# Cross attention with transposed scores, its output tiles spread over the iterations

## The reference, cut to what matters

```
def _attn(xq, ctx, wq, wkv, wo, bo):
    q = _heads(xq @ wq)
    k, v = jnp.split(ctx @ wkv, 2, axis=-1)
    ...
    q = _rope(q, sq, cq)
    k = _rope(k, sk, ck)
    sim = jnp.einsum('bhnd,bhmd->bhnm', q, k) * DH ** (-0.5)
    a = jax.nn.softmax(sim, axis=-1)
    o = jnp.einsum('bhnm,bhmd->bhnd', a, v)
    o = o.transpose(0, 2, 1, 3).reshape(xq.shape[0], xq.shape[1], MID)
    return o @ wo + bo
...
cross_in = _adaln(x, cond, ln1_w, ln1_b, g1_w, g1_b, b1_w, b1_b)
ctx_n = _ln(context, ca_lnc_w, ca_lnc_b)
x = _attn(cross_in, ctx_n, ca_wq, ca_wkv, ca_wo, ca_bo) + x
```

## Time and profile before

| what | us |
|---|---|
| median of three runs | 2480.38 |
| profiled execution, its own time | 2478.87 |
| its span | 2477.1 |
| PE busy | 2228.5 (90%) |
| DVE busy | 1860.5 (75%) |
| ACT busy | 1330.3 (54%) |
| POOL busy | 355.7 (14%) |

### The profile page before, as it was taken

One profiled execution on the slowest core, in us unless ns is written; L12 is line 12 of the kernel. 1 busy time (PEld: TensorE's weight loads), 2 busy tenths in 40 slices (PEclk: granted clock), 3 DMA queues, 4 the chain that ended last, 5 costly groups with the idle time before them and its releaser, 6 DMA issues. The chain is left out here.

```text
span 2477.1 us, 40034 instructions
## 1 busy us (share of the span) xinstructions
PE 2228.5 (90%) x15036; PEld 1042.1 (42%) x15036; DVE 1860.5 (75%) x2924; ACT 1330.3 (54%) x1655; POOL 355.7 (14%) x201
## 2 busy tenths in 40 slices
PE   2499999999999999999999999944899999994899
PEld 2133333344333344333334333442465656563566
DVE  6579989877989886899986998574766666666453
ACT  5266666755676654666664666443443443444221
POOL 3100000000000000000000000023554545452000
PEclk9699999999999999999999999967898999986899
DMA  5101010101111011101010110052322222224211
GB/s 163 54 35 36 35 44 35 39 32 44 52 40 40 27 44 44 52 27 44 35 44 35 52 36 27 19 160 72 94 85 85 85 85 85 85 85 128 67 38 34
DMA packets 106254, 143.81 MB, mean 58 GB/s; under 512 B 28209, under 2 KB 74367, under 8 KB 106111
## 3 DMA queue, kind: packets, MB, share of 16 engines
q1 hardware_dynamic: 106111, 141.87, 17.9%
HBM read 55.70 MB, written 12.85 MB: 28 GB/s over the span
## 5 line engine op out<-in xcount | busy, mean ns | idle before, releaser
L642 PE MATMUL sa_ps_o<-sa_probs,sa_v_pair 128*64 128x512 f32 x2048 | 532.7, 614 | 2.9 <-DVE sa_mx L897 2.9
L806 ACT ACTIVATE sa_probs<-sa_ps_s 128x1024 f32<-128x1024 f32 x512 | 495.8, 1025 | 27.9 <-PE sa_ps_s L629 27.9
L897 DVE CUSTOM_DVE_ANT_0 sa_rise<-sa_ps_t,sa_rise 128x512 f32<-128x512 f32 x504 | 327.9, 688 | 190.7 <-PE sa_ps_t L606 190.3
L910 DVE TENSOR_TENSOR sa_acc<-sa_acc,sa_probs 128x1024 f32<-128x1024 f32 x384 | 462.6, 1246 | 7.2 <-ACT sa_probs L806 7.2
L794 ACT ACTIVATE sa_rise<-sa_ps_t 128x1024 f32<-128x1024 f32 x252 | 257.7, 1023 | 250.0 <-PE sa_ps_t L599 250.0
L642 PEld LDWEIGHTS sa_ps_o<-sa_probs,sa_v_pair 128*64 128x64 f32 x2048 | 101.9, 134 | 246.4 <-issue 173.7
L576 POOL TENSOR_TENSOR sa_xr<-sa_xr,sa_bo_row 128x1024 f32<-128x1024 f32 x8 | 21.6, 2726 | 1280.1 <-DMA sa_xr<-in_x 1280.1
L622 PE MATMUL sa_ps_s<-sa_hi 64*128 64x512 f16 x1024 | 194.5, 376 | 0.0
L622 PE MATMUL sa_ps_s<-sa_hi,sa_lo 64*128 64x512 f16 x1024 | 194.4, 376 | 0.0
L622 PE MATMUL sa_ps_s<-sa_lo,sa_hi 64*128 64x512 f16 x1024 | 194.4, 376 | 0.0
L629 PE MATMUL sa_ps_s<-sa_m_line,sa_m_ones 64*128 64x512 f16 x1024 | 189.5, 377 | 3.7 <-DMA sa_m_line<-sa_m_rows 3.7
(11 more groups left out here) (275 smaller groups left out, 4613.5 us busy)
## 6 DMA issues: line engine op xcount, KB each, us to landing
sa_swp<-sa_raw SPq DMA_DIRECT2D x128, 256.0 KB, 2.4
ca_swp<-ca_raw SPq DMA_DIRECT2D x70, 256.0 KB, 2.4
sa_inv<-sa_scratch SPq DMA_DIRECT2D x128, 128.0 KB, 2.9
ca_q_hl<-ca_hi SPq DMA_DIRECT2D x68, 128.0 KB, 2.3
ca_q_hl<-ca_lo SPq DMA_DIRECT2D x68, 128.0 KB, 2.3
sap_xs<-in_x SPq DMA_DIRECT2D x4, 1024.0 KB, 7.1
sa_xr<-in_x SPq DMA_DIRECT2D x4, 1024.0 KB, 5.9
cap_xs<-x_after_self SPq DMA_DIRECT2D x4, 1024.0 KB, 7.2
```

Of the source, the lines that this page charges most:

```text
L642: ins = pe.matmul(ps_o[rows(x), half(c)], v_pair[:, kt, rows(x)], probs[:, kt % 2, c, half(x)], start=(kt == 0), stop=(kt == NK - 1))
L806: act.activation(probs[:, kt % 2, c, :], ps_s[c][:, :], ACT.Exp, scale=float(DH) ** -0.5).then_inc(s_p, 1)
L897: dve.tensor_tensor_reduce(out=larger, in0=max_banks(j, t)[:, half(x)], in1=larger, scale=1.0, scalar=-3.0e38, op0=ALU.add, op1=ALU.max, a ...
L910: dve.tensor_tensor(acc[:, c, :], before, probs[:, kt % 2, c, :], ALU.add).then_inc(s_acc[c], 1)
```

## The change

Cross attention is written anew in 32 unrolled iterations, one for each head pair g. The scores are made with the 77 keys on the partitions, both heads of the pair at once from 64 rows each (`scores`), so that probabilities need no transposing. The maxima come from separate products of the high parts with queries on the partitions (`bases`), one DVE instruction over 1232 columns, one transpose of 128 by 16, and one transfer into four lines; four products of 32 rows subtract them (`shift`). Sums come from four products with ones, and go through `few`, a scratch in memory and two transfers of 256 KB into `inv`; DVE divides the output. The rotation of q is on DVE alone. `swp` has one buffer instead of two. The values of pair g - 1 stand ahead of the transpose of g's maxima. One output tile of the batch before is made in each iteration from g = 11 on, with `o_hi` and `o_lo` two batches deep; three tiles and the last batch's eight follow the iterations. x is loaded and stored tile by tile, and its bias is added by POOL tile by tile. In the context stage the stacking transfers go, and the split keys are written where cross attention reads them; the key and value weights are freed ahead of cross attention.

```diff
-                sp.wait_ge(s_hi, n + 1)
-                for x in range(2):
-                    for dst in (k_hh[0:DH], k_hh[DH:P]):
-                        sp.dma_start(dst[:, half(n), x], hi[DH * x:DH * x + DH, half(n)]).then_inc(s_stack, 16)
-                sp.wait_ge(s_lo, n + 1)
-                for x in range(2):
-                    sp.dma_start(k_lo[:, half(n), x], lo[DH * x:DH * x + DH, half(n)]).then_inc(s_stack, 16)
-            sp.wait_ge(s_stack, 16 * 12)
+                sp.wait_ge(s_swap[n], 32)
...
-        ps_sc = ps("ps_sc", [P, TT, P])
-        ps_pt = ps("ps_pt", [P, N])
+        ps_s = ps("ps_s", [P, 2, N])
         ps_o = ps("ps_o", [P, N])
-        ps_turn = [ps(f"ps_turn{i}", [P, HALF]) for i in range(2)]
+        ps_t = ps("ps_t", [P, N])
+        turn = [ps_t[:, 0:HALF], ps_t[:, HALF:N]]
...
+        def output_tile(g):
+
+            return g - PAIRS - 3 if PAIRS + 3 <= g < PAIRS + 3 + TT * (B - 1) else None
+
+        def y_bank(n):
+            if n < TT * (B - 1):
+                later = n - output_tile(G)
+                return (turn[0] if later <= 0 else ps_s[:, 1, :] if later == 1 else turn[1])[:, 0:D]
+            t = n % TT
+            return (ps_s[:, t // 2, t % 2 * HALF:t % 2 * HALF + D] if t < 4 else turn[t - 4][:, 0:D] if t < 6 else
+                    ps_o[:, (t - 6) * HALF:(t - 6) * HALF + D])
+
+            def line(j):
+                sp.wait_ge(s_mt_r, j + 1)
+                sp.dma_start(m_line[0:P:32, :], m_rows[:]).then_inc(s_line, 16)
+
+            def gather_sums(g):
+                sp.wait_ge(s_sum_r, g + 1)
+                if g >= 1:
+                    sp.wait_ge(s_scr, 16 * g)
+                sp.dma_start(few[:], sums[0:P:32, :]).then_inc(s_few, 16)
+
+            def spread_inverses(g):
+                sp.wait_ge(s_rec, g + 1)
+                if g >= 1:
+                    sp.wait_ge(s_inv, 32 * g)
+                    sp.wait_ge(s_div, g)
+                sp.dma_start(scratch.rearrange("n (i k) -> (n i) k", k=16), few[:]).then_inc(s_scr, 16)
+                sp.wait_ge(s_scr, 16 * (g + 1))
                 for x in range(2):
-                    sp.dma_start(q_hl[0:DH, par, x, :], hi[DH * x:DH * x + DH, :]).then_inc(s_stack[par], 16)
-                sp.wait_ge(s_lo, j + 1)
-                for x in range(2):
-                    sp.dma_start(q_hl[DH:P, par, x, :], lo[DH * x:DH * x + DH, :]).then_inc(s_stack[par], 16)
+                    sp.dma_start(inv[rows(x), :], scratch[2 * x:2 * x + 2].rearrange("a k -> (a k)")
+                                 .partition_broadcast(DH)).then_inc(s_inv, 16)
+
+            def store(n):
+                sp.wait_ge(s_yr, n + 1)
+                sp.dma_start(y_v[n // TT][:, n % TT, :], xr[:, n % TT, :]).then_inc(s_out[n % 2], 16)
+
+            def load(n):
+                sp.wait_ge(s_out[n % 2], 16 * ((n - TT) // 2 + 1))
+                if n >= TT + 2:
+                    sp.wait_ge(s_xb, 2 + n - TT - 1)
+                sp.dma_start(xr[:, n % TT, :], x_v[n // TT][:, n % TT, :]).then_inc(s_x[n % 2], 16)
 
...
+            for g in range(G):
+                if g + 2 < G:
+                    swap(g + 2)
+                line(g)
+                n = output_tile(g - 1)
+                if n is not None:
+                    if n >= 2:
+                        load(n - 2 + TT)
+                    store(n)
+                if g >= 2:
+                    spread_inverses(g - 2)
+                if g >= 1:
+                    gather_sums(g - 1)
+            spread_inverses(G - 2)
+            gather_sums(G - 1)
+            spread_inverses(G - 1)
...
+            for h in range(2):
+                hs = slice(TT // 2 * h, TT // 2 * (h + 1))
+                pool.tensor_tensor(xr[:, hs, :], xr[:, hs, :], bo_row[:].broadcast_to([P, TT // 2, D]),
+                                   ALU.add).then_inc(s_xb, 1)
+            for n in range(TT, TT * B):
+                pool.wait_ge(s_x[n % 2], 16 * ((n - TT) // 2 + 1))
+                pool.tensor_tensor(xr[:, n % TT, :], xr[:, n % TT, :], bo_row[:, 0, :], ALU.add).then_inc(s_xb, 1)
 
...
+            def bases(g):
+                b, pair = g // PAIRS, g % PAIRS
                 for t in range(TT):
-                    ts = slice(t * P, (t + 1) * P)
-                    pe.matmul(ps_sc[:, t, 0:M], q_hl[:, par, x, ts], k_hh[:, pair, x, b, :], start=True, stop=False)
-                    ins = pe.matmul(ps_sc[:, t, 0:M], q_hl[0:DH, par, x, ts], k_lo[:, pair, x, b, :],
-                                    start=False, stop=True)
-                ins.then_inc(s_sc_w, 1)
-
-            def transposes(par, x):
-                for t in range(TT):
-                    ins = pe.transpose(ps_pt[0:M, t * P:(t + 1) * P], e[:, par, x, t, :], ident[:, :])
-                ins.then_inc(s_pt_w, 1)
+                    at = t // 4 * HALF + t % 4 * M
+                    for x in range(2):
+                        ins = pe.matmul(ps_s[:, x, at:at + M],
+                                        hi[rows(x), g % 3, t * P:(t + 1) * P], k_hi[rows(x), pair, b, :],
+                                        start=True, stop=True)
+                ins.then_inc(s_base, 1)
+
+            def scores(g):
+                b, pair, s = g // PAIRS, g % PAIRS, g % 3
+                for c in range(2):
+                    for n, (k, q) in enumerate(((k_hi, hi), (k_lo, hi), (k_hi, lo))):
+                        for x in range(2):
+                            pe.matmul(ps_s[0:M, c, half(x)], k[rows(x), pair, b, :], q[rows(x), s, half(c)],
+                                      start=(n == 0), stop=False)
+
+            def shift():
+                for x in range(2):
+                    for c in range(2):
+                        quarter = slice(32 * (2 * x + c), 32 * (2 * x + c) + 32)
+                        ins = pe.matmul(ps_s[0:M, c, half(x)], m_ones[quarter, 0:M], m_line[quarter, :],
+                                        start=False, stop=True)
+                ins.then_inc(s_st, 1)
+
+            def values(g):
+                b, pair = g // PAIRS, g % PAIRS
+                for c in range(2):
+                    pe.wait_ge(s_p, 2 * g + c + 1)
+                    if g >= 1:
+                        pe.wait_ge(s_oev, 2 * (g - 1) + c + 1)
+                    for x in range(2):
+                        at = pair * P + DH * x
+                        ins = pe.matmul(ps_o[rows(x), half(c)], v_all[:, b, at:at + DH], probs[:, c, half(x)],
+                                        start=True, stop=True)
+                    ins.then_inc(s_pv, 1)
+
+            def totals(g):
+                for c in range(2):
+                    for x in range(2):
+                        n = 2 * x + c
+                        ins = pe.matmul(turn[0][32 * n:32 * n + 32, :], ones32[0:M, 0:32], probs[:, c, half(x)],
+                                        start=True, stop=True)
+                ins.then_inc(s_sum, 1)
+
+            def output(n, ks, start, stop):
+                ts = slice(n % TT * P, n % TT * P + P)
+                return split_product(pe, y_bank(n), ks, (o_hi, o_lo), wo,
+                                     lambda k: (slice(None), (n // TT * PAIRS + k) % (2 * PAIRS), ts),
+                                     lambda k: (slice(None), k, slice(None)), start, stop)
 
...
+            for g in range(G):
+                pe.wait_ge(s_hi, g + 1)
+                if g >= 1:
+                    pe.wait_ge(s_p, 2 * g)
+                bases(g)
+                if g >= 1:
+                    values(g - 1)
+                pe.wait_ge(s_max, g + 1)
+                pe.wait_ge(s_q_r, 2 * min(g + 3, G))
+                pe.transpose(turn[1][0:2 * TT, 0:P], mx[:, g % 2, :], ident[:, :]).then_inc(s_mt, 1)
+                n = output_tile(g)
+                if n is not None:
+                    pe.wait_ge(s_ot, PAIRS * (n // TT + 1))
+                    pe.wait_ge(s_yr, n)
+                    pe.wait_ge(s_sum_r, g - 1)
+                    output(n, range(KM), True, True).then_inc(s_y, 1)
+                pe.wait_ge(s_lo, g + 1)
+                scores(g)
+                if n is not None:
+                    pe.wait_ge(s_yr, n + 1)
+                if g >= 1:
+                    if g >= 2:
+                        pe.wait_ge(s_sum_r, g - 1)
+                    totals(g - 1)
+                pe.wait_ge(s_line, 16 * (g + 1))
+                shift()
+                if g + 3 < G:
+                    pe.wait_ge(s_mt_r, g + 1)
+                    project(g + 3, 0)
+                    if g >= 1:
+                        pe.wait_ge(s_sum_r, g)
+                    project(g + 3, 1)
...
+            for g in range(G):
+                if g >= 1:
+                    evacuate_o(g - 1, 0)
+                row(g)
+                if g >= 1:
+                    evacuate_o(g - 1, 1)
+                if g >= 3:
+                    high_output(g - 3)
+                if g >= 1:
```

(33 more changed lines are left out.)

439 lines of the change are left out of this document (185 added, 254 removed).

## The result

The changed kernel takes 2343.9 us (median of four runs, 2340.9 to 2347.0) where the kernel before took 2479.7 on the same chip (2477.4 to 2482.9): a ratio of 0.9452, 95% interval 0.9434 to 0.9469. That is 135.8 us less; 115 had been forecast. The profiled execution took 2346.98 around a span of 2345.2, 131.9 less than the span of before.

A forecast was written before the change was run, and what follows sets the result against it. PE was taken to set the stage, with other engines idle while it projects. Cross attention's terms summed to 413.7 us against 521.9; with 7.2 from the context stage, 115.4 gained: 2365 us, likeliest 2350 to 2385, 8 in 10 within 2325 to 2415.

The forecast's parts named there:

- the chain: Tile iterations: totals wait for the residual, which stands behind ACT and low output at 6.55; 11.75 us before the allowance.
- head: Cross attention's start: swaps, rotations and POOL's bias addition, which delays DVE by up to 3.9; 24.0 us, nothing gained.
- pair 31 to its shift: Last loop iteration up to its subtraction of the maxima, forecast at 8.2 us.
- an iteration with a tile: Iterations 11 to 30, each with one output projection tile: 12.1 us each, 242.0 in all.
- the base products: PE's 16 products of 64 rows and 77 columns per iteration: 0.056 each, 0.9 us; bounds 0.45 and 2.24.
- the allowance for the low clock and for POOL: Added to each tile iteration for the low clock and POOL's bias additions beside DVE's work: 0.35 us.
- rival A: PE alone binds iterations with a tile: 11.1 us each, 20 us less, total 2336 to 2345; chance 0.17.
- Iterations without a tile: Iterations 3 to 10, bound by DVE's own work at 9.8 us each: 78.4 us.
- Iterations 0 to 2: First three iterations, with no division yet: 8.3 us each, 24.9 in all.
- B: Small tiles don't overlap: bases at 2.24 and shift at 0.86, 45 us more, 2410; chance 0.14.
- C: The line of maxima lands 3 us late through SP's queue: 24 us more, 2389; chance 0.13.
- D: Waits that DVE's order puts on PE keep it at 1.2 GHz: 260 us more, 2625; chance 0.03.

The follow-up runs named there:

- e1_residual: Changed kernel with VectorE adding the output tile to the residual before the low half of the output instead of behind it: 2333.8 us.
- e2_eighth: Changed kernel with the 21 output tiles inside the loop multiplying one eighth of the depth (3 products of 24): 2365.0 us.
- e7_head: Changed kernel with GpSimd's two bias additions in the stage's head waiting for the first rotation and the first maxima: 2339.4 us.
- e8_tail: Changed kernel with the output tile of iterations 29 to 31 moved behind the shift: 2332.6 us.
- e4_values_late: Changed kernel with the previous pair's values behind the transpose of the maxima, and ScalarE's row of maxima copied ahead of the output: 2426.1 us.
- e11_half: Changed kernel with the 21 output tiles inside the loop multiplying half of the depth (12 products of 24): 2356.0 us.
- e3_one_shape: Kernel before, with the keys' low half padded by zero rows so all 16 score products of a head have one shape: 2466.4 us, ratio 0.994.
- e5_order: Changed kernel with VectorE's first rotation product ahead of its wait for the high part, then residual, low output, rest of rotation: 2327.0 us.

## Why the prediction came out as it did

The sign and the chain held, and all terms but one came within 2.4 us; the total was 21 us too high. 2344 lies in the wide range, but outside the 2350 to 2385 that had the largest chance, 0.50. By the prediction's own terms, read from the trace:

| term | forecast | measured | off |
|---|---|---|---|
| context stage's gain | 7.2 | 6.7 | +0.5 |
| head | 24.0 | 22.4 | -1.6 |
| pairs 0 to 3 | 24.9 | 26.2 | +1.3 |
| pairs 3 to 11 | 78.4 | 76.0 | -2.4 |
| pairs 11 to 31 | 242.0 | 221.8 | -20.2 |
| pair 31 to its shift | 8.2 | 10.0 | +1.8 |
| tail | 36.2 | 36.8 | +0.6 |

*The term mis-sized.* Nearly the whole miss is in one row: an iteration with a tile, forecast at 12.1, took 10.98 in 18 of 20. Of the 1.12, 0.51 are the base products, taken at 0.9 from the nearest instruction in self attention when the bound of 0.45 was the better guess, as 0.39 shows. 0.35 is the allowance for the low clock and for POOL: the clock was 1.00, and the lengthened rotation (1.42 instead of 1.22 for its first product) lay in VectorE's slack. The residual came at T + 6.39 instead of 6.55, which is 0.16, and drains make up the rest. Iterations 29 and 30 took 10.9 and 13.2.

*The chain was right.* In the 18 iterations totals start right after the residual, for which TensorE waits 0.38; moving the residual alone shortened it (e1_residual), and taking work off TensorE did not (the 10.98 in e2_eighth). The time lies in rival A's 2336 to 2345, but not by A's mechanism; that is a coincidence of two bounds that lie close together. With bases measured, A's own figure of 11.1 would be 10.6, and e1_residual measured 10.54. Of the signs named, VectorE's idle time before its maximum was 0.86 and not 1.5 to 2, and the base products started 0.024 apart and not 0.056: the same mis-sized term.

*Iterations without a tile* were VectorE's, as forecast: no idle before the maximum, 9.49 against 9.8. The 0.3 are overlaps of neighbours, as most of the operations start 1.13 to 1.14 apart where I counted 1.2. *Iterations 0 to 2*, forecast at 8.3 each, took 10.03, 7.65 and 8.47; the first ran at a clock of 0.71, the other two at 1.00.

*Head.* The collision with POOL was placed rightly (e7_head); its price of up to 3.9 was 3.3, the same as e7_head got back. *Pair 31 and iteration 30* are what I left out: with no projection left to fill, TensorE waits 2.28 for the exponentials and in this execution loses the clock behind it (e8_tail fills the place).

*Rivals.* B (shapes don't overlap) fell: shifts and bases both ran beside each other. Its 0.14 was the alternation alone. C (the line comes late) did not happen. The line was there at about T + 4.2, forecast 4.1: with a tile the shift never waits for it, and ahead of the tiles TensorE waits 0.8 to 0.9 for it in nine iterations, which from pair 3 on VectorE's 9.49 covers. D, the low clock, did not bind in this kernel: two of the eight iterations without a tile ran at 0.82 and still took 9.49. Yet its mechanism is real: e4_values_late, e2_eighth and e11_half have it. What kept it away is the place of the values and the whole tile in the loop, as these runs show. I gave D 3% on the means of the kernel before; the means don't tell how near a kernel stands to that edge.

By the figure in the Trainium skill, "TensorE: Matmul & The Clock Gate", section Back-to-back issue gap, about 81 ns a product with 128 columns, bases would have cost 1.3, an estimate; the trace has 0.39, so it does not agree and the measurement decides. The same page of the Trainium skill, section Part 4: PE-mode transpose, says that transposes don't count as TensorE's activity for the clock, from which the prediction worked out that the clock rises when they go. It rose, from 0.91 to 0.96, but e3_one_shape leaves the transposes as they were and the clock falls to 0.78, so no run here isolates that rule.

Two things stay open. No run tells when a wait is followed by a fall of the clock: waits of 1.54, 2.28 and 2.67 us had one behind them in some iterations and none in others. And the share of the first eight iterations in the clock's 50 us of e4_values_late is an estimate, as none of them ran at full clock.

## What to carry to other kernels

Before an edit gives TensorE less to do or moves work behind a wait, ask what fills the hole: here less work in the loop cost 12 to 21 us and a hole of 1.5 us in each iteration 82, more than half of it through the clock, while moving work into holes gained 11 us (e8_tail) and 17 (e5_order). Find which of two neighbouring bounds sets an iteration before you shorten either, since the next one may lie 0.4 us behind. Keep products of one shape together and let those on different rows take turns; on a TensorE that has waits besides, as in e3_one_shape, expect little of the time back.
